# Four conditioned sequence layers in one kernel: convolution on TensorE, softplus from |x|, smaller helper matmuls

## The reference

```python
xm, z = jnp.split(h @ W_in, 2, axis=-1)             # 512 channels each
xc = conv_general_dilated(xm^T, conv_w, (1,), [(3, 0)], feature_group_count=512)   # 4 taps per channel
xm = silu(xc + conv_b)
dtr, Bm, Cm = jnp.split(xm @ W_xp, [64, 80], axis=-1)
dt = softplus(dtr @ W_dt + b_dt)
# per position t:  h = h * exp(dt_t * A) + (dt_t * x_t) * B_t ;  y_t = sum over 16 states of h * C_t
y = (ys + xm * D_param) * silu(z)
out = x + gate * (y @ W_out)
```

## Time and profile before

| | |
|---|---|
| median of 3 runs | 5616.87 us |
| profiled execution, own time | 5616.71 us |
| its span, first to last instruction | 5614.9 us |
| busy VectorE / TensorE / GpSimd / ScalarE | 87% / 79% / 73% / 62% |
| mean granted TensorE clock | 0.901 |
| instructions | 66460 |

### The profile page before, as it was taken

How to read it: one execution, slowest core, us unless ns; L and a number is a source line. 1 busy time by engine, 2 the same in 40 slices (tenths; PEclk the granted TensorE clock), 3 DMA queues, 4 the chain that set the end, 5 groups by cost and what they waited for, 6 DMA issues and landing times.

```text
span 5614.9 us, 66460 instructions
## 1 busy us (share of the span) xinstructions
PE 4463.3 (79%) x15736; PEld 2300.2 (41%) x15736; DVE 4895.1 (87%) x5146; ACT 3463.0 (62%) x6182; POOL 4077.3 (73%) x2847
## 2 busy tenths in 40 slices
PE   4577888888788878888888888888788888888755
PEld 1233344444444434444444444444444444444323
DVE  3749999999999999999999999999999999999482
ACT  2346666667666666766666666766666676766352
POOL 2728787877878877777877777777877777787272
PEclk8678899999999999999999999999999899998775
DMA  4516666666667666666666666666666666666161
GB/s 143 193 64 232 213 231 214 225 219 207 233 202 228 225 219 221 212 229 201 224 225 221 218 219 224 207 227 212 222 212 223 219 210 228 214 228 209 63 209 51
DMA packets 350275, 1147.58 MB, mean 204 GB/s; under 512 B 38790, under 2 KB 79275, under 8 KB 349835
## 3 DMA queue, kind: packets, MB, share of 16 engines
q1 hardware_dynamic: 305674, 1088.05, 58.7%
q10 hardware_dynamic: 44160, 54.60, 3.1%
HBM read 1123.47 MB, written 19.04 MB: 203 GB/s over the span
## 4 chain that ended last, share of the span: by engine, by line
POOL 41%; issue 26%; DVE 12%; PE 10%; DMA 5%; ACT 4%; POOLq 1%; SPq 1%; DVEq 0%; ACTq 0%
POOL hw L984 30%; POOL hw L991 8%; DVE hw L966 5%; DMA cs<-bc_scratch 3%; DVE ps L952 3%; DMA bs<-bc_scratch 2%; PE ps L1139 1%; POOL rstd L611 1%; POOL dtx L840 1%; DVE u L796 1%; PE ps L853 1%; PE ps L677 1%; PE ps L1056 1%; PE ps L1148 1%; PE ps L1131 1%
## 5 line engine op out<-in xcount | busy, mean ns | idle before, releaser
L984 POOL TENSOR_TENSOR hw<-hw,cs 128x1024 f32<-128x1024 f32 x1024 | 2419.6, 2363 | 887.9 <-DVE hw L966 824.6
L966 DVE TENSOR_TENSOR_SCAN hw<-da,ps 128x1024 f32<-128x1024 f32 x1024 | 2334.2, 2279 | 59.7 <-ACT da L902 20.0
L902 ACT ACTIVATE da<-dt,a_neg 128x510 f32<-128x510 f32 x2048 | 1331.3, 714 | 359.9 <-DVE hw L966 357.8
L952 DVE TENSOR_TENSOR ps<-ps,bs 128x1024 f32<-128x1024 f32 x1024 | 1254.5, 1225 | 138.2 <-DMA bs<-bc_scratch 85.5
L991 POOL TENSOR_TENSOR hw<-hw 128x512 f32<-128x512 f32 x1024 | 1301.2, 1271 | 70.8
L853 PE MATMUL ps<-hw,ident 128*128 128x512 f32 x2048 | 1139.3, 663 | 129.1 <-POOL hw L991 128.8
L672 PE MATMUL ps<-hT,w_in 128*128 128x512 f32 x1024 | 532.6, 656 | 209.2 <-ACT sz L774 117.8
L853 PEld LDWEIGHTS ps<-hw,ident 128*128 128x128 f32 x2048 | 389.0, 208 | 571.3 <-issue 293.3
L1313 ACT ACTIVATE pts<-ps,mcur 128x256 f32<-128x256 f32 x1024 | 401.0, 476 | 251.6 <-PE ps L1236 249.8
L549 ACT ACT_TABLE_LOAD x353 | 452.9, 1283 | 54.7 <-issue 48.6
L1347 DVE TENSOR_REDUCE mx<-ps 128x2 f32<-128x512 f32 x512 | 330.0, 678 | 81.8 <-PE ps L1207 80.9
(11 more groups left out here) (186 smaller groups left out, 5994.1 us busy)
## 6 DMA issues: line engine op xcount, KB each, us to landing
bs<-bc_scratch SPq DMA_DIRECT2D x1024, 512.0 KB, 5.0
cs<-bc_scratch SPq DMA_DIRECT2D x1024, 512.0 KB, 4.1
xhat<-in_x ACTq DMA_DIRECT2D x16, 512.0 KB, 4.4
gate<-gates_scratch ACTq DMA_DIRECT2D x64, 128.0 KB, 4.7
x_b<-in_x ACTq DMA_DIRECT2D x16, 512.0 KB, 7.3
x_scratch<-x_b ACTq DMA_DIRECT2D x16, 512.0 KB, 2.9
x_c<-x_scratch ACTq DMA_DIRECT2D x16, 512.0 KB, 5.5
out<-x_c ACTq DMA_DIRECT2D x32, 256.0 KB, 2.5
```

The lines of the kernel that those rows point to most:

```text
L902: ins = nc.scalar.activation(da[q % (AHEAD + 1)][:, k, :, 1:S], dt_[:, c, :].rearrange("p (b s) -> p b s", b=GB)[:, :, 1:S], ACT.Exp, scal ...
L952: nc.vector.tensor_tensor(z, dxp.unsqueeze(1).broadcast_to([P, 2, T]), bs[s % B_RING][:, :, :], ALU.mult)\
L966: nc.vector.tensor_tensor_scan(tile[:, :, :].rearrange("p n t -> p (n t)"), da[s % (AHEAD + 1)][:, :, :, :].rearrange("p n b s -> p (n b s)"),
L984: nc.gpsimd.tensor_tensor(tile[:, :, :], tile[:, :, :], cs[s % C_RING][:, :, :], ALU.mult)\
```

## The change

1. Convolution on TensorE. ScalarE copies the projected chunk to `u`; TensorE multiplies it by four diagonal matrices (one for each tap, shifted outputs, accumulated in a PSUM bank); ScalarE applies silu with the bias from PSUM to `u`. The 32 diagonal matrices are made at the start, kept in DRAM, and 1 MB of them (one layer's) is loaded by SyncE in every front into one shared buffer `taps`.
2. dt = max(x, 0) + ln(1 + exp(-|x|)). The bias b_dt comes through an extra row of `w_dt` and a row of ones in `xd` (97 rows instead of 64). ScalarE takes |x| from PSUM (`abs_dt`); VectorE's cap is gone; its last instruction for dt stays, with other operations.
3. Bias rows: two rows (rounded part and remainder) and a column pair of ones in the format of one pass, instead of one 32-bit row.
4. The mask matmul takes 64 rows (0 to 63 for the even, 64 to 127 for the odd bank) instead of 128; the head selection takes 32 rows instead of 128.
5. All positions in `PLACES` are new.

The core of the diff:

```diff
 def front_piece(sem, name):
-    pe = ["h0", "h1"] + [f"m{m}" for m in range(IC)] + ["xp", "d0", "d1"]
+    pe = ["h0", "h1", "m0", "m1", "c0", "m2", "c1", "c2", "m3", "c3", "xp", "d0", "d1"]
...
     "front0": {
-        "pe": [27.467, 27.633, 27.8, 27.967, 28.133, 28.55, 28.8, 29.05, 30.467, 30.633, 30.8, 31.133],
-        "act": [24.35, 26.35, 26.6, 26.85, 28.211, 28.322, 28.433, 28.544, 28.656, 28.767, 28.878, 29.35, 29.6,
-               29.85],
-        "dve": [26.165, 26.247, 29.382, 29.433, 29.485, 29.536, 29.588, 29.639, 29.691, 29.742, 29.794, 29.845,
-               29.897, 29.948, 30.553, 31.082, 31.165, 31.247],
+        "pe": [23.8, 24.05, 24.5, 24.7, 24.9, 25.1, 25.6, 25.9, 26.2, 27.5, 27.7, 27.9, 28.1, 28.8, 29.633,
+               29.967],
+        "act": [20.767, 21.671, 21.814, 21.957, 22.6, 23.7, 23.9, 25.6, 27.6, 28.6, 29.267, 29.433, 29.6,
+               29.767, 29.933],
+        "dve": [21.665, 21.832, 31.58, 31.83, 32.08],
+        "pool": [22.425, 31.8, 32.05, 32.3],
+        "sp": [24.033, 30.6, 31],
     },
     "front1": {
-        "pe": [24.8, 25.05, 25.54, 25.78, 26.02, 28.8, 30.55, 30.675, 30.8, 30.925, 31.175, 32.05],
+        "pe": [19.8, 20.05, 20.633, 20.8, 20.967, 21.8, 22.8, 25.7, 26.1, 27.467, 27.633, 27.8, 27.967, 28.133,
+               28.55, 28.8],
+        "act": [19.386, 19.529, 19.671, 19.814, 19.957, 20.6, 23.3, 23.7, 26.6, 27.6, 28.6, 29.267, 29.433,
+               29.767, 29.933],
+        "dve": [18.732, 18.866, 30.777, 31.082, 31.165],
+        "sp": [15.867, 29.867, 30.533],
     },
...
+            pe.wait_ge(pc.of("xc0"), pc.upto(g, "xc0"))
+            pe.wait_ge(taps_in[l], 16 * g + 16)
+            convolve(pc, 0)
+            yield
+            project_in(l, pc, 2)
...
+        def convolve(pc, m):
+            bank = side[pc.bank[f"c{m}"]].rearrange("p (b s) -> p b s", b=GB)
+            xm = u[:, m, :].rearrange("p (b s) -> p b s", b=GB)
+            for s in range(TAPS):
+                ins = nc.tensor.matmul(bank[:, :, s:], taps[:, m, (TAPS - 1 - s) * P:(TAPS - s) * P],
+                                       xm[:, :, 0:S - s], start=(s == 0), stop=(s == TAPS - 1),
+                                       skip_group_check=True)
+            ins.then_inc(pc.next(f"c{m}"), 1)
...
-            nc.tensor.matmul(side[pc.bank[f"d{m}"]], w_dt[l][:, m * P:(m + 1) * P], xd[0:DTR, :],
+            nc.tensor.matmul(side[pc.bank[f"d{m}"]], w_dt[l][:, m * P:(m + 1) * P], xd[:, :],
...
-                nc.scalar.activation(u[:, m, :], side[pc.bank[f"m{m}"]], ACT.Identity,
-                                     bias=col(f"m{l}_conv_b", m), scale=col(f"m{l}_conv_w", m * TAPS + TAPS - 1))\
-                  .then_inc(pc.next(f"tap{m}"), 1)
+                nc.scalar.activation(u[:, m, :], side[pc.bank[f"m{m}"]], ACT.Copy).then_inc(pc.next(f"xc{m}"), 1)
...
+            nc.scalar.activation(dt_[:, m, :], side[pc.bank[f"d{m}"]], ACT.Abs).then_inc(pc.next(f"ab{m}"), 1)
...
-            for m in range(IC):
-                for s in range(1, TAPS):
-                    nc.vector.scalar_tensor_tensor(
-                        out=um[:, :, s:], in0=bank[:, :, 0:S - s], scalar=col(f"m{l}_conv_w", m * TAPS + TAPS - 1 - s),
-                        in1=um[:, :, s:], op0=ALU.mult, op1=ALU.add).then_inc(pc.next(f"cv{m}_{s}"), 1)
...
-            nc.vector.tensor_scalar(dt_[:, m, :], side[pc.bank[f"d{m}"]], col(f"m{l}_b_dt", m), EXP_CAP,
-                                    ALU.add, ALU.min).then_inc(pc.next(f"mn{m}"), 1)
...
         def front_sync(sp, l, g, prev):
+            taps_are_free(sp, l, g)
+            sp.dma_start(taps[:, :, :], taps_dram[l]).then_inc(taps_in[l], 16)
+            yield
...
-                                         pick[:, 0:1].broadcast_to([P, P]),
-                                         mb[:, :].unsqueeze(1).broadcast_to([P, 2, S]), start=True, stop=False,
+                                         pick_mask[rr, 0:1].broadcast_to([64, P]),
+                                         mb[rr, :].unsqueeze(1).broadcast_to([64, 2, S]), start=True, stop=False,
...
-                             row.unsqueeze(1).broadcast_to([1, RB, D]), start=True, stop=False,
+                             row.unsqueeze(1).broadcast_to([2, RB, D]), start=True, stop=False,
```

More of the change, by code:

```diff
@@ L570, in load_mask_row @@
         def load_mask_row(act, n):
-            for k in range(2):
-                act.dma_start(mb[32 * k:32 * k + 1, :].bitcast(F32), mask_dram[k, bass.ds(n, 1), :]).then_inc(min_, 16)
+            for half in range(2):
+                act.dma_start(mb[64 * half:64 * half + 2, :].bitcast(F32),
+                              mask_dram[:, bass.ds(n, 1), :].rearrange("k o s -> k (o s)")).then_inc(min_, 16)
         def load_key_mask(act, n):
@@ L742, in front_scalar @@
             wait_near(act, "rest", "d3")
-            nc.scalar.activation(xd[:, :], side[pc.bank["xp"]][0:DTR + 2 * NS, :], ACT.Copy).then_inc(pc.next("xd"), 1)
+            nc.scalar.activation(xd[0:DTR + 2 * NS, :], side[pc.bank["xp"]][0:DTR + 2 * NS, :], ACT.Copy).then_inc(pc.next("xd"), 1)
             if l == 1:
                 keep_result(act, g)
+            yield
+            for m in range(2):
+                abs_dt(act, pc, g, m, "scan")
             yield
@@ L816, in step_size @@
             nc.vector.scalar_tensor_tensor(
-                out=dt_[:, m, :], in0=side[pc.bank[f"d{m}"]], scalar=col(f"m{l}_b_dt", m),
-                in1=dt_[:, m, :], op0=ALU.add, op1=ALU.max).then_inc(pc.next(f"dt{m}"), 1)
+                out=dt_[:, m, :], in0=side[pc.bank[f"d{m}"]], scalar=0.0,
+                in1=dt_[:, m, :], op0=ALU.max, op1=ALU.add).then_inc(pc.next(f"dt{m}"), 1)
         def rest_vector(dve, l, g, prev):
             for m in (2, 3):
-                cap(dve, l, rs[l], g, m, "before")
-                yield
                 step_size(dve, l, rs[l], g, m)
@@ L1621, in _ @@
             loads = [(c_raw, a["c_t"].rearrange("(k p) b -> p k b", p=P)), (cols[:, :], a["cols"]),
[L1622 removed]
+                     (row_stage, a["rows"])]
             for k in range(5):
@@ L1652, in _ @@
             sp.dma_start(kmask_dram, key_rows).then_inc(masks_out, 16)
+            sp.wait_ge(p_taps, 1)
+            for l in range(2):
+                sp.dma_start(taps_dram[l], taps_stage[l][:, :, :]).then_inc(taps_out, 16)
+            sp.wait_ge(p_rows, 1)
+            for k in range(2):
+                sp.dma_start(rows_dram[k], qhl[0:len(ROWS), k, 0, :].bitcast(F32)).then_inc(rows_out, 16)
+            sp.wait_ge(rows_out, 32)
+            for r in range(len(ROWS)):
+                sp.dma_start(rows[32 * (r % 4):32 * (r % 4) + 2, r // 4, :].bitcast(F32), rows_dram[:, r, :])\
+                  .then_inc(rows_in, 16)
+            sp.wait_ge(taps_out, 32)
             all_iterations(sp, "sp")
@@ L1667, in _ @@
                                          base=0, pattern=[[-1, P]], channel_multiplier=1))
-            step(nc.gpsimd.memset(pick_f, 0.0))
+            step(nc.gpsimd.memset(yT[:, 3, 0:2 * NS + 1], 0.0))
+            for half in range(2):
+                step(nc.gpsimd.memset(yT[64 * half:64 * half + 2, 3, 2 * NS:2 * NS + 1], 1.0))
+            for l in range(2):
+                step(nc.gpsimd.memset(w_dt[l][DTR:DTR + 2 * NS, :], 0.0))
+            step(nc.gpsimd.memset(xd[DTR + 2 * NS:DTR + 2 * NS + 1, :], 1.0))
             for off in (0, 32):
```

254 lines of the change are left out of this document (144 added, 110 removed), and 15 rows, old and new, of the table PLACES.

## The result

| | before | after |
|---|---|---|
| median of 4 runs each, same chip | 5623.62 us (5615.27 to 5633.03) | 5734.98 us (5723.95 to 5741.41) |
| profiled execution, its span | 5614.9 us | 5733.6 us |
| first dbx of the first scan | 114.3 us | 136.7 us |
| first to second scan | 275.1 us | 288.0 us |
| one iteration, mean of the 14.5 between the second scan and the last but one | 322.8 us | 328.4 us |

The change makes the kernel slower: ratio 1.0199, 95% interval 1.0176 to 1.0223. The forecast was 5471 us with a range of 5300 to 5590, so both are wrong, and so is the sign. The 118.7 us between the two spans are 22.4 at the start, 12.9 in the first scan, 14.5 x 5.5 = 80 in the even stretch and 3.4 after it. The even stretch ends at 5070.67 us with the first dbx of the last scan but one; the earlier trace rows calls that scan the last, but the last one starts at 5357.2 us.

What follows compares the result with a forecast made beforehand. The prediction took VectorE, busy for 94% of the even stretch, to set the pace. 5616.7 us less 352 removed, plus 172 given back, 14 at the start and 20 for fronts without scans gave 5471 us, range 5300 to 5590.

Steps and rivals of the forecast that it cites:

- What is removed: VectorE's convolution (17.1 us), cap (5.9) and a decay wait (1.4) go: 24.4 us an iteration gained, 352 us in all.
- Term 1, front0: End of segment 1: front0's longer chain over TensorE leaves VectorE idle, 8 us an iteration, bounds 0 and 15.
- scans that wait for decays or reduces, some 7 us: Expected sign in segment 1 from step 24 on, some 7 us in sum, while TensorE runs without a gap.
- First decay wait: At an iteration's first step the scan's wait for its decay goes: 1.4 us an iteration gained.
- Term 2, light steps: Steps with little side work, 29 of 64 instead of 14, wait for B loads: 2.4 us an iteration, bounds 0 and 6.
- Term 3: End of segment 0: front1's chain ends about a quarter step late, 1 us an iteration, bounds 0 and 4.
- Term 4, taps: Loading the diagonals in each front delays the B load behind: 0.5 us an iteration, bounds 0 and 6.4.
- the rival on ring order: Rival, chance 0.06: B loads on SyncE wait for all bytes of the diagonals ahead, 6.4 us an iteration; 5555 us.
- TensorE and ScalarE: Work added beside other work: TensorE 286 and ScalarE 222 of 312 us an iteration, hidden except where order matters.
- under 15 us in all: Rival: one-pass bias rows and half masks not quicker, 10.7 us of TensorE an iteration; 0.03 for an unchanged result.
- Start and fronts without scans: Making and writing diagonals at the start costs 14 us; longer fronts with no scan beside them cost 20 us.
- The slower rival: Rival, chance 0.10: the front's chain on TensorE holds up the scan in both segments, 5.6 us an iteration lost; 5732 us.

Runs made afterwards that it cites:

- e10: Kernel before without VectorE's 24 convolution operations an iteration, nothing in their place, all places as before: 5548.77 us, ratio 0.9847.
- e7: Kernel before with dt from |x| on ScalarE and no cap on VectorE, convolution and places as before: 5637.89 us, ratio 1.0022.
- e9: Changed kernel loading the 1 MB of diagonals only for the first front, 4 KB in each later front: 5734.74 us, ratio 1.0194.
- e5: Changed kernel's operations under the places of the kernel before, two of front1's matmuls moved later: 6067.98 us, ratio 1.0797.
- e1: Changed kernel with front0's two copies of h and first three chunk copies on ScalarE behind the copy of chunk 3: 5685.36 us, ratio 1.0118.
- e2: Changed kernel with front0's two dt operations on VectorE moved ahead of scan 31: 5701.40 us, ratio 1.0141.
- e4: Changed kernel with the edits of e1 and e2, and decay 2 of segment 1 ahead of rest1's gates and back0's gate loads: 5736.72 us, ratio 1.0202.

## Why the prediction was wrong, point by point

- **"What is removed": the failed step.** 24.4 us of VectorE's time an iteration were counted as gained in full, because VectorE was busy for 94%. The instructions did go: the lengths of all VectorE instructions add up to 23.3 us an iteration less, as counted (17.1 + 5.9). Its busy time fell by 18.0 only, since records of instructions that follow each other directly overlap, and fewer do now. But above all, time on VectorE was not time of the kernel. Work taken off it shortened the iteration by 3.5 of 15.4 us in e10 (5.0 at most by the medians) and gained nothing in e7, which is 12 us slower. In the changed kernel VectorE's waits rose by 24.7 us an iteration, where the prediction gave back 11.9. High busy time was no proof that the time was set by it: where the removed instructions stood at the end of a segment, another engine's chain ran beside them, and they were cover.
- **Term 1, front0: 8 us.** The chain's length was right in kind: m0 to the end of xp is 25.2 us at the start against 23.2 worked out. The place was missed. I followed the decays behind the front's copies, but not the copy of chunk 3, which stands at 23.5 on the same engine; that alone is 9.6 us at step 24, where I had put nothing. From step 25 to step 30 the waits are 1.0 us in sum, against my "scans that wait for decays or reduces, some 7 us".
- **"First decay wait" gained.** At the iteration's first step it is gone, as forecast. But another came: scans wait for decays 12.4 us in four iterations, 5.6 before. The refit put three gates of rest1 and back0's loads ahead of decay 2 of segment 1. There VectorE waits 5.0 us at step 2, 2.9 of them for the decay and 2.1 for reduces. I had not followed this stage.
- **Term 2, light steps: 2.4 us.** The waits for B rows rose from 5.65 to 16.3 us an iteration, and I said more than 8. Half of the rise (5.8 us at dbx of step 2 in segment 0, nothing there before) is not light steps but the turn of the loop on GpSimd, 8.5 to 10.7 us from branch to next operation instead of 3.1 to 5.1, which I had not looked at. My "turn of the hardware loop 2.3" was VectorE's.
- **Term 3** held: at the end of segment 0 (steps 24 to 31) the waits are 3.8 us in sum, each small, against 1.2 before. **Term 4, taps**: 0 within the noise, not 0.5; the rival on ring order, with its 6.4 us an iteration, falls with it (e9).
- **TensorE and ScalarE.** The convolution is 455.5 / 16 = 28.5 us an iteration (27.5 worked out, from 0.43 us a record; 5.42 / 12 in the earlier trace rows is 0.45, which gives 28.9). Bias rows save 188.9 - 85.9 = 103.0 us in all, 6.4 an iteration (6.7), the masks 2.8 (4), 8 times |x| cost 4.8 (4.8). The head selection was left out of the sum: 5.1. The other sizes were right, their consequence was not: what was put at "under 15 us in all" was 42, head selection included. Nor did the sum look at the granted clock, which went from 0.901 to 0.886.
- **Start and fronts without scans.** 14 + 20 us forecast. Measured: 22.4 at the start, 12.9 in the first scan, 3.4 from the last scan but one to the end: 38.7. At the start the input load is 11.1 us later (14 worked out), and the first front from h0 to the first dbx takes 41.7 us against 30.0. So this part was right in size.
- **The slower rival** gave 5732 us, and 5735 came; that the two agree is luck. Its mechanism (both segments end late on TensorE's chain) is what e5 shows, not what the changed kernel does.

Of the 5.5 us an iteration that are lost, e1 gives back 4.1 by the order of the copy and e2 2.4 by an earlier branch of GpSimd. The two alone were not run together; e4, which holds both, speaks against their adding up. e1 is still 1.2% slower than before. Open is why the remaining waits of e1 are as they are: after it, VectorE still waits 20 us an iteration more than before for 18 us less work, in waits of 1 to 3 us at reduces, decays and B rows and in the 6.5 us of the loop's turn.

## What to carry to other kernels

Before taking work off the busiest engine, leave it out in its place and time that: it costs one run, and tells what its absence is worth in that order, before anything is added elsewhere. When a stage moves forward in a fixed order, follow on each engine every instruction that now stands behind it, the scan's rare ones (one in eight steps) as well as those of every step. A chain over several engines that ends just in time looks like a busy engine, because that engine's other work fills the wait. When a part is left out to see what it costs, look at the granted clock too: it can fall with the work and hide the gain.
